# A sixth weight unit placed in attention buffers, with a re-ordered dispatch tail, a new slot layout and constants loaded ahead

## The reference

```python
h = concat([tok(x), txt], axis=1)                     # 32 x 96 x 192, signs and a patch product
h = h + attention0(layernorm(h))                      # 12 heads of 16
h = h + soft_moe(layernorm(h))                        # 64 slots
h = h + attention1(layernorm(h))                      # one head of 192, rotary, causal
h = h + experts(layernorm(h))                         # 8 experts, top 2, relu
```

```python
xn = rms_norm(x, norm_weight); tok = l2_normalize(xn)
sl = l2_normalize(slots) * scale[:, None]             # 64 x 192
logits = einsum('sd,btd->bst', sl, tok)
dispatch_w, combine_w = softmax(logits, -1), softmax(logits, -2)
y = einsum('btd,bst->bsd', xn, dispatch_w)            # each slot gathers its input
y = gelu(einsum('sio,bsi->bso', fc1_weight, y) + fc1_bias)   # 64 x (192 x 768), one per slot
y = einsum('sio,bsi->bso', fc2_weight, y) + fc2_bias         # 64 x (768 x 192)
out = einsum('bsd,bst->btd', y, combine_w)
```

## Time and profile before

| what | us |
|---|---|
| median of three runs | 986.32 |
| profiled execution, and its span from first to last instruction | 984.93, 983.1 |
| attention0: slot tail after the last batch's values | 291.3 to 315.8 |
| slot_ffn: first matmul to the end of VectorE's transpose | 316.2 to 487.6 |
| combine with the layer norm's scale | 487.9 to 507.4 |
| attention1: first issue on SP, first matmul | 508.9, 514.2 |
| attention1, route and expert tiles to the end | 514.2 to 983.1 |

### The profile page before, as it was taken

One profiled execution on the slowest core, in us unless ns is written; L12 is line 12 of the kernel. 1 busy time (PEld: TensorE's weight loads), 2 busy tenths in 40 slices (PEclk: granted clock), 3 DMA queues, 4 the chain that ended last, 5 costly groups with the idle time before them and its releaser, 6 DMA issues. The chain is left out here.

```text
span 983.1 us, 24044 instructions
## 1 busy us (share of the span) xinstructions
PE 781.6 (79%) x8360; PEld 655.7 (67%) x8361; DVE 569.4 (58%) x1401; ACT 425.3 (43%) x1055; POOL 361.9 (37%) x389
## 2 busy tenths in 40 slices
PE   2489999999986656565559988952489999999993
PEld 2368888888865443343436766742479999999993
DVE  1727878778752211111466888868946565656562
ACT  4436776666741211111104776545234444444441
POOL 1323444443321000000003667624765555555552
PEclk8758999999975887788858999975589999999998
DMA  9391000000001999999329000016113332323331
GB/s 281 80 427 44 3 2 2 2 2 2 2 1 34 354 427 427 424 425 429 158 65 421 1 1 0 1 44 176 49 41 54 50 53 47 53 50 49 54 48 20
DMA packets 34037, 118.09 MB, mean 120 GB/s; under 512 B 7522, under 2 KB 24324, under 8 KB 29476
## 3 DMA queue, kind: packets, MB, share of 16 engines
q1 hardware_dynamic: 23108, 104.30, 27.6%
q0 software_dynamic: 10848, 12.67, 8.0%
HBM read 105.77 MB, written 11.14 MB: 119 GB/s over the span
## 5 line engine op out<-in xcount | busy, mean ns | idle before, releaser
L1694 POOL DMA_INDIRECT out_h<-x_ys,idx x55 | 87.5, 1591 | 97.5 <-ACT x_ys L1719 89.2
L1818 PE MATMUL psum<-w_pairs,x_h_hi 128*128 x330 | 101.8, 370 | 1.6 <-DVE x_h_lo L1746 1.1
L1820 PE MATMUL psum<-w_pairs,x_h_lo 128*128 x330 | 82.8, 251 | 0.0
L1069 PE MATMUL psum<-flat,yT 64*32 64x384 f32 x672 | 47.7, 658 | 38.1 <-issue 36.8
L1746 DVE TENSOR_TENSOR x_h_lo<-psum,x_h_hi 128x384 fp32r<-128x384 f32 x110 | 56.2, 552 | 36.9 <-ACT x_h_hi L1715 36.9
L1270 POOL MEMSET b_ones<- 96x96 f32 x1 | 0.2, 179 | 201.3 <-POOLq L138 201.3
L538 POOL TENSOR_SCALAR a_u<-flat,a_mv 96x192 f32<-96x192 f32 x32 | 24.2, 757 | 133.5 <-DVE a_mv L675 133.5
L1719 ACT ACTIVATE x_ys<-x_ys,cw 128x192 f32<-128x192 f32 x55 | 25.1, 456 | 104.2 <-DVE x_ys L1757 104.2
L1818 PEld LDWEIGHTS psum<-w_pairs,x_h_hi 128*128 128x128 f32 x330 | 61.9, 188 | 3.8 <-issue 3.8
L1715 ACT ACTIVATE x_h_hi<-psum 128x384 fp32r<-128x384 f32 x110 | 48.0, 489 | 35.4 <-PE psum L1807 32.2
L1820 PEld LDWEIGHTS psum<-w_pairs,x_h_lo 128*128 128x128 f32 x330 | 62.9, 191 | 0.1
(11 more groups left out here) (265 smaller groups left out, 2283.1 us busy)
## 6 DMA issues: line engine op xcount, KB each, us to landing
flat<-in_slot_w SPq DMA_DIRECT2D x27, 2304.0 KB, 26.3
m_ring_last<-in_slot_w SPq DMA_DIRECT2D x5, 2304.0 KB, 27.0
flat<-in_moe_w SPq DMA_DIRECT2D x1, 10752.0 KB, 29.2
flat<-in_x_patches SPq DMA_DIRECT2D x4, 1536.0 KB, 15.0
out_h<-flat SPq DMA_DIRECT2D x1, 2304.0 KB, 12.2
xtab<-flat SPq DMA_DIRECT2D x4, 576.0 KB, 4.0
m_y<-in_fc_b SPq DMA_DIRECT2D x4, 384.0 KB, 12.5
x_xg<-xtab,idx POOLq DMA_INDIRECT x55
```

The lines of the kernel that those rows point to most:

```text
L1069: mm = pe.matmul(b_h[n][r][B * c:B * (c + 1), :], g.yT[rows, k, SC * gr + c, :], w1[c // 2][rows, c % 2, k, n * N2:(n + 1) * N2], start=(k ...
L1694: pool.indirect_dma_start(out=A["out"][:, :], out_offset=bass.IndirectOffsetOnAxis(ap=g.idx[:, i:i + 1], axis=0), in_=ys[:, i % 2, :], in_ ...
L1818: pe.matmul(b_y[u % 2], h_hi[:, k, :], g.w_pairs[:, :, k, bass.ds(e, 1), :].rearrange("p two a d -> p two (a d)"), start=(k == 0), stop=False)
L1820: mm = pe.matmul(b_y[u % 2][:, 1, :], h_lo[:, k, :], g.w_pairs[:, 1, k, bass.ds(e, 1), :].rearrange("p a d -> p (a d)"), start=False, stop ...
```

## The change

Four things change together.

1. The buffers p, vv and kT of attention0 now lie in the sixth ring slot, which is allocated for both stages. SP loads the sixth unit at the end of attention0's list, after the last scores, the last transposes and the last values. To make room, `dm` and `dT` have one buffer instead of two; the waits in `dispatch_max` and `scale_turned` are one chunk tighter.
2. For the last chunk (`END`) the slot work uses the PSUM banks that the finished attention leaves: its products go one batch at a time to bank 3 (`last_product`), the transposes to banks 1, 4 and 5. The last batch's three `turn`s use banks 6, 4 and 5. The gather of the last but one chunk goes ahead of the transpose of the last logits, and the last gather ahead of the last `turn_combine`.
3. `y2` and `y2T` have the slots (the batches) innermost.
4. The six constants of attention1 go into a buffer of their own and are issued by SP at the end of slot_ffn's list.

```diff
+                g.ring.append(small0("ring_last", [128, UNIT])[:, :])
...
+        last = g.ring[NU - 1]
+        p = last[0:T, 0:n_p].rearrange("p (i h t) -> p i h t", i=2, h=NH)
+        vv = last[0:T, n_p:n_p + n_vv].rearrange("p (i h d) -> p i h d", i=4, h=NH)
+        kT = last[0:HALF, n_p + n_vv:UNIT].rearrange("p (i m a t) -> p i m a t", i=2, m=2, a=2)
...
-        dm = sb("dm", [NS, 2, CH, T])
-        dT = sb("dT", [T, 2, CH, NS])
+        dm = sb("dm", [NS, CH, T])
+        dT = sb("dT", [T, CH, NS])
...
             for n in range(NU - 1):
                 load_unit(sp, A, g, n)
+            sp.wait_ge(s_sc, B)
+            sp.wait_ge(s_pTp, NG * B)
+            sp.wait_ge(s_oTp, B)
+            load_unit(sp, A, g, NU - 1)
...
+            y_copy(END)
+            turned_copy(END)
...
-                if q >= 2:
-                    v.wait_ge(s_dTp, q - 1)
+                if q >= 1:
+                    v.wait_ge(s_dTp, q)
...
-                if q >= 2:
-                    v.wait_ge(s_yp, q - 1)
+                if q >= 1:
+                    v.wait_ge(s_yp, q)
...
-                    if b or r:
+                    if b == B - 1:
+                        pe.wait_ge(s_pTs, b * NG)
+                    elif b or r:
                         pe.wait_ge(s_pTs, b * NG + r)
...
+            def last_product(b):
+                n = b - END * CH
+                if n < 0:
+                    return
+                pe.wait_ge(s_sub, B)
+                pe.wait_ge(s_xTs, b + LAG + 1)
+                mm = product(END, n)
+                if n == CH - 1:
+                    mm.then_inc(s_raw, 1)
...
             def turn_dispatch(q):
                 pe.wait_ge(s_d, q + 1)
-                pe.wait_ge(s_dsub, q + 1)
-                if q >= 1:
-                    pe.wait_ge(s_ys, q)
+                if q == END:
+                    pe.wait_ge(s_pTs, NG * B)
...
-                if q + 1 < NQ:
+                if q + 2 < NQ:
                     pe.wait_ge(s_dsub, q + 2)
+                elif q + 2 == NQ:
+                    pe.wait_ge(s_cTs, q + 1)
                 else:
-                    pe.wait_ge(s_cTs, q + 1)
+                    pe.wait_ge(s_lg, q + 1)
...
-        g.y2 = sb("y2", [128, SH, HALF])
-        g.y2T = g.ring[2][:, 0:B * HALF].rearrange("p (b d) -> p b d", b=B)
+        g.y2 = sb("y2", [128, HALF, SH])
+        g.y2T = g.ring[2][:, 0:B * HALF].rearrange("p (d b) -> p d b", b=B)
...
-            load_unit(sp, A, g, NU - 1)
...
+            load_attention1(sp, A, g)
...
-                rows = g.y2[:, 4 * gr:4 * gr + 4, :]
+                rows = g.y2[:, :, 4 * gr:4 * gr + 4].rearrange("p d s -> p s d")
...
-            v.transpose(g.y2T.rearrange("p b d -> p d b"), g.y2[:, :, :].rearrange("p s d -> p d s")).then_inc(s_y2T, 1)
+            v.transpose(g.y2T.rearrange("p d b -> p (d b)"), g.y2[:, :, :].rearrange("p d s -> p (d s)")).then_inc(s_y2T, 1)
...
-                    mm = pe.matmul(g.ps[0:T, 2 * (b % NB) + half, 0:HALF], g.combT[rows, b, :], g.y2T[rows, b, :],
+                    mm = pe.matmul(g.ps[0:T, 2 * (b % NB) + half, 0:HALF], g.combT[rows, b, :], g.y2T[rows, :, b],
```

## The result

The changed kernel takes 976.42 us (median of 4 runs, 974.56 to 978.64), the kernel before 987.26 us beside it (984.41 to 991.48). Over the single runs the ratio is 0.9888, with a 95% interval of 0.9845 to 0.993. The profiled execution took 974.56 us, 10.4 us less than that of before.

The account below looks back on a forecast made before the run. Slot_ffn was taken as bound by its weight stream, the stretches around it by engine chains. 1.2 + 5.6 + 1.8 + 3.5 = 12.1 us off 984.93 left 972.8, or 974.2 by the median; forecast 973.5, range 970 to 977.

Parts of the forecast that it names:

- The tail: Dispatch tail ahead of slot_ffn: product groups cost 1.5 us, later steps leave the chain; net gain 1.2 us.
- the third rival: Dispatch tail: the 1.5 us of product groups stay and nothing is won behind; 975.5 us, chance 0.11.
- The single dm and dT: Attention0: their tighter waits cost nothing, since TensorE does the named matmuls earlier in its own order anyway.
- The sixth unit: Slot_ffn's weight stream: one unit moves to an idle stretch beside the tail; gain 5.6 us, ends 0 and 6.5.
- The second rival: Slot_ffn: the weight stream gains nothing, as the ring only waits for slots; 978.4 us, chance 0.12.
- Slots innermost: End of slot_ffn: big transpose 2.1 us shorter, one strided add 0.34 longer; net gain 1.8 us, combine counted as nothing.
- The fourth rival: Combine becomes bound by TensorE's strided read, so the kernel is slower; 993.6 us, chance 0.06 with anything like it.
- The constants: Attention1's constants issued at the end of slot_ffn's list: TensorE starts 5.1 us earlier; net gain 3.5 us.
- the new wait: Attention1, batch 8: ScalarE waits 1.9 us for the expert weights, of which 1.6 us count as loss.
- The first rival: Attention1: the wait for the expert weights is absorbed by idle time; gain 13.7 us, 971.2 us, chance 0.15.
- in front of nothing that slot_ffn waits for: End of slot_ffn's list: constants behind the last unit take under 2 us of an idle queue.
- the prediction's own sign: Forecast is wrong if stages up to attention1's first matmul shorten by under 10 us, or the gain is lost behind.

Follow-up runs that it names:

- moe_first: Changed kernel with the expert weights as SP's first issue in attention1, ahead of the four small transfers: 972.54 us, ratio 0.9851.
- tail_old: Changed kernel with the dispatch tail's old PSUM banks and old order, the sixth unit still loaded early: 978.24 us, ratio 0.992.
- ring_const: Changed kernel with the sixth unit loaded in slot_ffn again and the constants issued when the last second product is done: 976.83 us, ratio 0.9911.
- const_behind: Changed kernel with the six constants issued only when the last second product is done: 972.86 us, ratio 0.9877.
- ring_late: Changed kernel with the sixth weight unit loaded at the start of slot_ffn again: 978.07 us, ratio 0.992.
- after_again: The changed kernel itself, unaltered, run once more in more rounds: 974.18 us, ratio 0.9898.
- const_late: Changed kernel with the six constants issued in attention1's own block again: 976.41 us, ratio 0.9915.
- both: Changed kernel with the edits of moe_first and const_behind together: 971.59 us, ratio 0.9847.
- all_three: Changed kernel with the edits of both, and the last gather but one behind the last logits' transpose: 968.62 us, ratio 0.9822.

## Why the prediction held, point by point

**The tail (forecast -1.2).** Its steps are to be compared at the same clock: moe_first against before, each from its third last input transpose (282.63 above, 282.91 here), behind which the clock is half in both.

```profile
282.91 0.55 PE L805 MATMUL psum<-ident,a_u 96*96 96x96 f32 x2 [0.74 <-POOL a_u L540]
...
316.22 6.82 PE L1069 MATMUL psum<-flat,yT 64*32 64x384 f32 x96 [1.31 <-PEq L431]
```

From there the last input transpose comes 1.0 us later (forecast 1.5), the logits' transpose 0.8 later (1.4), `turn_dispatch` 0.8 earlier (0.2), slot_ffn's first product 2.05 earlier (1.2; 2.1 against tail_old). The mechanism is right, the third rival is not; the size is short by 0.85, of which 0.5 lie ahead of the last input transpose. From the first weight issue the same two runs differ by 1.4 only, since before's full clock began 1.3 us sooner behind that issue, which is worth 0.6. One step of the prediction does not come out of its own rows: 302.18 + 1.5 - 0.79 - 2.1 is 300.8 and not 301.3. Of the 0.79 only 0.28 went, as the product then waits 0.51 us for the copy of the input, and 301.3 was right. The single dm and dT cost nothing, as forecast: from the fifth to the thirtieth input transpose both runs take 175.47 us.

The prediction left out a term: the granted clock can come back inside the tail, and in the profiled execution of the changed kernel that gave 3.3 us more. One program showed 0, 3.4 and 6.8 us of full clock there. Whether these 3.3 us belong to the change is open: old order, none in 2 profiles; new order, some in 6 of 12. The 12 sort by when the full clock of attention0 had begun: 31.2 to 31.9 us behind the first weight issue, 6.8 us again; 32.6, 3.4 us; 33.1 to 34.5, none. The two of the old order, 31.6 and 32.6, lie among those with some, and had none. So the order may have a part in it; two profiles don't show it.

**The sixth unit (-5.6).** 5.5 to 5.7 by ring_const and before. The second rival, no gain, falls: the last product waited for its transfer in every run. What the sum lacked is the clock at that product. Where it had waited 1.78 us (before) or 1.44 (ring_const) it took 2.19 us; in the other runs it had waited 2.8 to 5.0 us and took 3.2 to 4.1, wholly or in part at half clock. In the profiled execution that is 1.9 us: -5.6 + 1.1 for the constants + 1.9 - 1.7 for the layout are the -4.3 of the stage.

**Slots innermost (-1.8).** 1.7. The fourth rival, the slower one, falls: combine kept its length, with no idle time on VectorE behind the first add. The Trainium skill's rule on memory lines (Advanced Engine Details and Errata, section Memory Cachelines) was weighed there as the sign of a loss. The trace agrees with it for VectorE's adds (919 ns instead of 558) and shows next to none of it on TensorE (387 ns instead of 379).

**The constants (net -3.5).** The gain, 5.1, measured 4.94. The loss by the new wait, 1.6, is right as long as the clock holds: const_behind, ring_late, after_again and ring_const wait 1.78 to 2.33 us and have 145.9 to 146.1, moe_first, const_late, both and all_three hardly wait and have 144.2 to 144.5. The first rival, the absorbed wait, falls.

Two steps failed. The first is the sentence that the issues stand "in front of nothing that slot_ffn waits for": transfers that are issued behind another still took part of its time, 1.1 us; the last two products are 6.68 us apart with them and 5.33 without. (The Trainium skill, DMA: Bandwidth & Descriptors, section Queues, rings and completion order, says that each transfer engine takes its descriptors in order, but that a later one may be written before an earlier; the trace agrees that order in the queue is no shield: three of the six constants landed ahead of the unit that was issued ahead of them.) The second is that a wait costs only its length: in the four runs where a stretch of half clock (3.4 or 6.8 us) followed in the middle of attention1, the stage took 147.1 to 148.8, 1 to 3 us more. The loss lies behind the wait: all eight runs that waited took the first piece of the expert weights 30.7 to 31.3 us behind the stage's first matmul, however long the wait (29.0 to 29.1 in the four that hardly waited), and from there those four take 115.8 to 117.6 us, the other four 114.9 to 115.4. All four had waited 2.0 to 3.3 us for the weights, and no run without the wait had such a stretch; that the wait brings it on is likely by that, not shown, since four other runs waited about as long without it. Net of the part in the profiled execution: 4.98 - 3.92 - 1.1, nearly nothing.

**Sum.** The profiled executions differ by 10.4 us where 12.1 were summed, and the median lies 2.9 us above the forecast. It came that near because the full clock behind the third last transpose (3.3), what came ahead of that transpose (0.2 in attention0, 0.7 ahead of the first weight issue) and the 0.85 that the order won beyond the forecast paid for most of what the last unit (1.1 and 1.9), attention1 (2.3 more than forecast) and the last stages (1.2) lost. As far as the runs show, the part of the clock is luck: the tail, the unit and the layout were right in their mechanism, but the closeness of the total is not their merit. By the prediction's own sign, 15.5 us were won up to attention1's first matmul, and 5.2 of them lost behind it. The 1.2 us in route and expert tiles are scatter: that stretch is 323.8 to 325.3 us over all the runs.

## What to carry to other kernels

A load that is put "behind" the stream still shares the transfer engines with the last unit that the stage waits for; start it when that unit's consumer is done, if the next stage leaves it the time. When a front wait is removed from a stage, look for the load that this stage overlaps, and issue that first. Before crediting an edit with a gain in a stretch where the granted clock changes, run the same instructions again, and compare between two points where the clock is the same: here a mark that lay 236 us ahead of the edited steps mixed in 0.6 us from the start of the stage.

## What the runs showed of the hardware that was not expected

- One and the same instruction list (the programs differ only behind it) ran the end of attention0 in three clock patterns: half clock (1.2 GHz) from 279 to 282 on, then full (2.4 GHz) for 0, 3.4 or 6.8 us, then half until slot_ffn has begun. From the first weight issue to slot_ffn it took 267.7 to 268.3, 265.6 and 263.4 to 264.0 us, from the third last input transpose 31.3, 29.5 and 27.7 to 28.0.
- Behind the last input transpose the length repeated to 0.01 us: 15.16 or 15.17 in ten runs, 13.48 and 13.49 with the edit that shortened it. A stretch at one clock tells edits apart that the total, with some 0.4% between runs, doesn't.
- Transfers queued behind a unit lengthened that unit: 6.5 to 7.2 us between the last two products with the constants in the queue and the unit early, 5.0 to 5.5 without.
